# Order of the mixing and value products, order of two gathers, and packed table indices in a four-layer attention and adapter kernel

## Time and profile before

| | |
|---|---|
| median of three runs | 425.72 us |
| the profiled execution, its own time | 422.87 us |
| its span, first to last instruction | 421.1 us |
| TensorE (PE) busy | 409.3 us, 97% |
| VectorE (DVE) busy | 308.1 us, 73% |
| GpSimd (POOL) busy | 258.2 us, 61% |
| ScalarE (ACT) busy | 240.8 us, 57% |
| the 16 DMA engines, mean busy share in the main loop | 0.58 |

### The profile page before, as it was taken

How to read it: one execution, slowest core, us unless ns; L and a number is a source line. 1 busy time by engine, 2 the same in 40 slices (tenths; PEclk the granted TensorE clock), 3 DMA queues, 4 the chain that set the end, 5 groups by cost and what they waited for, 6 DMA issues and landing times.

```text
span 421.1 us, 9975 instructions
## 1 busy us (share of the span) xinstructions
PE 409.3 (97%) x2942; PEld 315.8 (75%) x2942; DVE 308.1 (73%) x901; ACT 240.8 (57%) x611; POOL 258.2 (61%) x230
## 2 busy tenths in 40 slices
PE   5999999999999988999999999999999999999997
PEld 1586877888945566888787878878778778888776
DVE  3798768769478586967978779687786787967742
ACT  4383433433267465756767567666676666765741
POOL 3206775275579877777777777777767777662000
PEclk9999999999999999999999999999999999999999
DMA  6616565157584455656555656565565655653321
GB/s 177 218 51 195 170 179 182 53 168 260 157 267 119 149 148 149 180 154 175 163 138 166 169 161 165 140 180 156 147 177 141 171 160 137 186 144 99 109 69 61
DMA packets 74107, 65.15 MB, mean 155 GB/s; under 512 B 50277, under 2 KB 52453, under 8 KB 74055
## 3 DMA queue, kind: packets, MB, share of 16 engines
q1 hardware_dynamic: 55088, 38.09, 31.3%
q0 software_dynamic: 15456, 22.08, 19.7%
q10 hardware_dynamic: 3510, 4.35, 2.9%
HBM read 74.46 MB, written 11.93 MB: 205 GB/s over the span
## 4 chain that ended last, share of the span: by engine, by line
PE 82%; DMA 5%; DVE 4%; POOL 4%; issue 4%; ACT 1%; SPq 0%; POOLq 0%; DVEq 0%; ACTq 0%
PE banks L1151 37%; PE banks L1141 11%; PE banks L1315 11%; PE banks L1294 9%; PE banks L1331 4%; PE banks L1167 3%; PE banks L1354 3%; PE banks L1344 2%; DMA wpt_late<-newkv,idx_all 1%; DMA newkv<-kvo 1%; POOL q_roots L497 1%; POOL wpt_late L524 1%; POOL windows L524 1%; DMA windows<-newkv,idx_all 1%; DMA xt_s<-xt_dram 1%
## 5 line engine op out<-in xcount | busy, mean ns | idle before, releaser
L524 POOL DMA_INDIRECT windows<-kvrows_dram,idx_all x78 | 83.0, 1064 | 31.1 <-issue 24.0
L524 POOL DMA_INDIRECT windows<-newkv,idx_all x78 | 81.8, 1049 | 29.0 <-issue 22.6
L655 ACT ACTIVATE pt_s<-banks 112x384 f32<-112x384 f32 x128 | 56.0, 496 | 61.9 <-PE banks L1141 56.9
L649 ACT ACTIVATE prob<-prob,negmax 128x336 f32<-128x336 f32 x128 | 72.4, 566 | 24.4 <-DVE negmax L1011 24.4
L1011 DVE CUSTOM_DVE_ANT_0 prob<-banks,mask 128x336 f32<-128x336 f32 x128 | 57.4, 503 | 2.7 <-PE banks L1294 1.2
L1021 DVE TENSOR_SCALAR prob<-prob,rinv 128x336 f32<-128x336 f32 x128 | 47.1, 410 | 2.3
L1294 PE MATMUL banks<-kt_s,qt_s 64*128 64x336 f32 x256 | 44.8, 468 | 0.0
L1315 PEld LDWEIGHTS banks<-pt_s,windows 112*64 112x64 f32 x624 | 33.3, 136 | 13.4 <-issue 10.9
L1315 PE MATMUL banks<-pt_s,windows 112*64 112x128 f32 x624 | 42.7, 279 | 0.0
L1151 PE MATMUL banks<-wf_hi,x 128*128 128x512 f32 x120 | 41.1, 403 | 0.0
L1141 PE MATMUL banks<-ident_r,prob_w 128*112 128x128 f32 x384 | 40.4, 242 | 0.0
(11 more groups left out here) (222 smaller groups left out, 918.2 us busy)
## 6 DMA issues: line engine op xcount, KB each, us to landing
usel<-utab SPq DMA_DIRECT2D x64, 128.0 KB
xt_s<-xt_dram SPq DMA_DIRECT2D x16, 256.0 KB, 3.7
newkv<-kvo SPq DMA_DIRECT2D x16, 256.0 KB, 2.6
stage<-xtok_dram SPq DMA_DIRECT2D x16, 256.0 KB, 11.3
tsel<-ttab SPq DMA_DIRECT2D x64, 64.0 KB
out_dram<-xo ACTq DMA_DIRECT2D x15, 256.0 KB
windows<-kvrows_dram,idx_all POOLq DMA_INDIRECT x78
windows<-newkv,idx_all POOLq DMA_INDIRECT x78
```

The costliest lines, as they stand in the source:

```text
L524: P.indirect_dma_start(kv_s[i][:, c, :], None, newkv if new else kvrows, bass.IndirectOffsetOnAxis(ap=idx_all[:, new * CH + c, b:b + 1], a ...
L649: A.activation(pr, pr, ACT.Exp, bias=negmax[:, g:g + 1], scale=-1.0, accum_out=psum_p[b % 2][:, g:g + 1]).then_inc(S["exp_done"], 1)
L655: A.activation(pt_s[g][:], tb[g % 2][0:KP, 0:CH * 128].rearrange("p (c q) -> p c q", c=CH), ACT.Copy).then_inc(S["pt_ev"], 1)
```

## The change

TensorE: `values` becomes one call with both halves, and in even stages `mix` moves ahead of it. GpSimd: the new rows of sequence k+3 are fetched at the head of turn k, where those of sequence k+2 were; the wait on `comb_ev` at k = 0 moves behind `gather(3, 1)`. SyncE: one number a tile holds subject, `ad2` and `ad3` of both sequences and is taken apart in registers; VectorE makes these numbers once in `meta`, with two instructions more than before.

```diff
@@ SyncE, load_tile
                 after(sp, S["l1_mm"], t - 1)
+                both = sp.value_load(picks[0:1, t:t + 1], min_val=0, max_val=PICKS * PICKS - 1)
+                pick = [both % PICKS, both // PICKS]
                 for u in range(2):
-                    s = sp.value_load(subj_s[0:1, 2 * t + u:2 * t + u + 1], min_val=0, max_val=7)
+                    s = pick[u] % 8
...
-                    a2 = sp.value_load(ad2_s[0:1, 2 * t + u:2 * t + u + 1], min_val=0, max_val=NE2 - 1)
-                    a3 = sp.value_load(ad3_s[0:1, 2 * t + u:2 * t + u + 1], min_val=0, max_val=NE3 - 1)
-                    a23 = sp.value_load(pair_s[0:1, 2 * t + u:2 * t + u + 1], min_val=0, max_val=NE2 * NE3 - 1)
+                    a23 = pick[u] // 8
+                    a2, a3 = a23 % NE2, a23 // NE2
@@ GpSimd, the loop
             for k in range(NB):
-                if k == 0:
-                    pool.wait_ge(S["comb_ev"], NE3 // 2)
-                    gather(4, 0)
-                    continue
-                if k + 2 < NB:
-                    gather(k + 2, 1)
+                if k + 3 < NB:
+                    gather(k + 3, 1)
                 if k + 4 < NB:
-                    pool.wait_ge(S["pv_mm"], k)
+                    if k == 0:
+                        pool.wait_ge(S["comb_ev"], NE3 // 2)
+                    else:
+                        pool.wait_ge(S["pv_mm"], k)
                     gather(k + 4, 0)
@@ VectorE, meta
                 V.tensor_copy(adf[:, 0, :], ad2_s[:])
-                link(V.tensor_copy(adf[:, 1, :], ad3_s[:]))
-                link(V.scalar_tensor_tensor(adf[:, 2, :], adf[:, 1, :], float(NE2), adf[:, 0, :], ALU.mult, ALU.add))
-                V.tensor_copy(pair_s[:], adf[:, 2, :]).then_inc(S["meta_ready"], 1)
+                V.tensor_copy(adf[:, 1, :], ad3_s[:])
+                link(V.tensor_copy(adf[:, 2, :], subj_s[:]))
+                link(V.scalar_tensor_tensor(adf[:, 0, :], adf[:, 1, :], float(NE2), adf[:, 0, :], ALU.mult, ALU.add))
+                link(V.scalar_tensor_tensor(adf[:, 2, :], adf[:, 0, :], 8.0, adf[:, 2, :], ALU.mult, ALU.add))
+                two = adf[:, 2, :].rearrange("a (t u) -> a t u", u=2)
+                V.scalar_tensor_tensor(picks[:], two[:, :, 1], float(PICKS), two[:, :, 0], ALU.mult, ALU.add).then_inc(S["meta_ready"], 1)
@@ TensorE, values (both halves in one call) and the even stage
-            def values(b, p):
+            def values(b):
...
+                for p in range(2):
+                    pe.wait_ge(S["pt_ev"], 4 * b + 2 * p + 2)
...
                     scores(n)
-                    values(k, 0)
                     if t >= 1:
                         mix(t - 1)
-                    values(k, 1)
+                    values(k)
```

More of the change, by code:

```diff
@@ L149, in build @@
         adf = sb("adf", [1, 3, NB])
-        pair_s = sb("pair_s", [1, NB], i32)
+        picks = sb("picks", [1, TILES], i32)
+        PICKS = 8 * NE2 * NE3
         pos = sb("pos", [128, TILES])
@@ L1309, in values @@
                     pe.wait_ge(S["wf_ev"], 1)
[L1310 to L1318, removed]
+                for p in range(2):
+                    pe.wait_ge(S["pt_ev"], 4 * b + 2 * p + 2)
+                    for c in range(CH):
+                        for h in range(2):
+                            g = 2 * p + h
+                            col = 256 * u + 128 * p
+                            last = mm(ob[64 * h:64 * h + 64, col:col + 128], kv_s[b % WINDOWS][:, c, 256 + 64 * g:320 + 64 * g],
+                                      pt_s[g][:, c, :], start=(c == 0), stop=(c == CH - 1))
+                last.then_inc(S["pv_mm"], 1)
             def project(t):
```

## The result

The changed kernel takes 535.55 us (median of four, 533.23 to 538.75) against 425.95 us before: a ratio of 1.2586, 95% interval 1.2498 to 1.2674. Forecast were 526 us and a range of 476 to 565. All ratios here leave out executions that lie more than 1.5% above the fastest of the same kernel; the medians count every execution.

What follows compares the result with a forecast made beforehand. PE bounded the loop at 8.65 us a stage; after the change POOL would: 152.0 us to the first second pass, 27 turns of 12.34, then issue, landing and PE's 27.7 gave span 520.7, scaled to 526 us, range 476 to 565.

Steps and rivals of the forecast that it cites:

- PE bounds the loop, POOL is next: Loop of 26 stages: PE busy without a hole, 8.65 us a stage; POOL's six gathers fill 8.2 us of it.
- The gather order: POOL's loop: the second pass waits right behind its own first pass; a turn becomes 12.34 us against 8.65.
- W: Time from the end of the third old-row DMA's instruction to the first new-row one: between 2.0 and 6.13, taken as 4.5 us.
- The first second pass: POOL's first wait in the loop: reached at 147.5 us, W of 4.5, so `gather(4, 1)` starts at 152.0.
- Another price for the wait: Skill page's DMA formula: 2.5 us for 112 rows of 2 KB, W some 2.8, sum below 477 us.
- Mixing and packing: PE's joined `values` spare 2.4 us in 15 even stages, SP's packed indices are off the path; both booked at 0.
- the rival of the free wait: POOL's loop: W stays below 0.8 us and POOL keeps PE's pace; 421 us, chance 0.04.
- signs in PE's share: PE waits for new-row DMAs before `keys_t` about 100 us in total; its share falls to some 78%.
- Quiet queue: Rival on POOL's gathers: old rows land as in the early phase, W = 2.9; 480 us, chance 0.22.
- Full load: Rival on POOL's gathers: table loads still keep the slowest DMA engine busy, W = 6.13; 572 us, chance 0.12.
- The clock: Rival on PE: stages run at 1.2 GHz, loop 450 us, kernel about 680; chance of clock beyond the wait 0.02.

## Why the prediction was right, step by step

**PE bounds the loop, POOL is next.** Right in the profile that it was read from, and incomplete: the `usel` loads were a third at the same pace. A loop without a hole on PE shows what is the bound, not how near the next one is. Nothing in the waits of that execution named `usel`; it took a kernel that spares PE or SP a little time to make it show. One sign was there: SP waited for nothing between 160 and 400 us, and the loads of one tile stretched over 16.0 of its 17.3 us. A queue that is worked off in order and never waits has no slack to show, whichever engine the profile puts in front.

**The gather order.** Right in its mechanism, shown by doing it alone (534.13 us) and by undoing it (434.90). The mis-sized term is W: 4.5 forecast, 5.36 measured. Its picture, one gather of a tile under SP's table loads and one without, is what the chain of waits of the changed kernel shows (the third old-row DMA of a turn from issue to landing):

```profile
291.43 7.27 DMA windows<-kvrows_dram,idx_all
...
305.94 4.28 DMA windows<-kvrows_dram,idx_all
...
317.71 6.24 DMA windows<-kvrows_dram,idx_all
```

but both are longer than forecast: POOL's idle time is 4.25 us on average in the odd turns and 6.48 in the even ones, for 2.9 and 6.13, so the quieter half was the worse guess. A turn took (502.14 - 152.62) / 27 = 12.94 us, from the second pass of sequence 4 to that of 31, for 12.34 forecast: 27 x 0.6 = 16 us more. W alone makes some 25 of it; the gather instructions were shorter than their mean before (1.01 for 1.06 us), which took some 9 back. The first second pass began at 152.62, forecast 152.0. That it is so close is luck: POOL came to that wait at 149.18 instead of 147.5, and the wait was 3.44 instead of 4.5. From the last one to the end it was 535.4 - 502.14 = 33.3 us, forecast 35.5, because the last rows landed sooner. The profiled execution was 537.21 us and lay 1.7 above the median, where a scaling from the execution before had added 3.5. Together 16 + 0.6 - 2.2 - 5.2 = 9.2, close to 535.55 - 526 = 9.55. So the total is nearer than W, since errors of both signs stand in it.

**Another price for the wait.** The measured waits decide against the formula of the Trainium skill, "DMA: Bandwidth & Descriptors", section "Anatomy of one DMA — SWDGE (gpsimd) path", for these gathers (2.0 us plus bytes / 436e3): 3.81 us on average even with the split loads, where the prediction had worked out some 2.8 from it. The rule on the number of engines, from the section named above of the same page of the Trainium skill, agrees with the packets: two at a time before the split, up to 16 after it.

**Mixing and packing.** Booked at 0, they are 0 in the sum, because POOL hides them; alone they are not. For the packing I had argued that SP's time is off the path, because its waits list nothing and its tile of 17 us ends within PE's 17.3. That is the step that was wrong: alone it costs 8 us (434.37). With split loads the ratios with and without it are 0.9948 and 0.9886, some 2.6 us, and, with the two `root_queries` moved, 0.9881 and 0.9869, some 0.5 us; the intervals of both pairs overlap, so what is left of its cost stays open. Why its denser issue makes `usel` land later was not isolated; that the loads go about two packets at a time, and that the split takes the wait away, is shown. For the same reason the rival of the free wait had a wrong price, 421: without the gather order the change is at 434.90. The signs in PE's share were off as well, 82% for 78% and 84 us of waits for 100: a part of the wait was filled with work at half clock.

**The rivals.** Quiet queue: nearest with the split loads, at 3.81 us, and not in the changed kernel. Full load: half of the turns. The clock: it falls behind PE's waits, to 0.67 over a whole turn of POOL at the lowest, and by the waits it costs nothing while POOL is the bound. Its price of 680 us does not follow from its own 450: with 450 in the place of 224.82 the kernel would take some 651. The Trainium skill, "TensorE: Matmul & The Clock Gate", section "Part 1: The HAM clock gate", says that an idle array is throttled to half rate, and the trace agrees: 0.50 granted behind a wait of 5.0 us.

## What to carry to other kernels

Before moving an instruction on an in-order engine, name the instruction that will stand right ahead of it: a wait that was met long ago can turn into the full latency of what was issued just before, and its price is latency times turns, however idle the engine looks on the page. A bound that shows no hole may have a second one within one per cent, and an in-order queue that never waits is the place to look; a small gain on the first is then worth nothing until the second is found, here by the name in the waits of a kernel that was meant to be faster. Here a DMA that repeats a source through a leading dimension of 2 was worth splitting.

## What the runs showed of the hardware that was not expected

- An old-row pass of three indirect DMAs (up to 112 rows of 2 KB each) landed 7.3, 4.3 and 6.2 us after the issue of its third in three turns in a row of the same kernel, at a DMA share of 0.40 over the loop.
- Splitting the 128 KB `usel` load in two took its packets from about two at a time to up to 16, the longest issue on SP from 4.8 to 1.7 us in the kernel before, and the wait for another queue's gathers from 5.36 to 3.81 us in the changed kernel.
- A wait of 5 us on PE was followed by 3 us at half clock (0.50 granted). In a kernel that PE bounds, one late load cost a wait of 2.8 us and then 4.18 for 2.99 us of dense work behind it.
